# Decoder of two layers, self-attentions: the maxima carried to the query rows by halves, exponentials 12 slots behind

## What is computed

```python
# layer 0: 16 heads of 16, causal
scores = jnp.einsum('bhqd,bhkd->bhqk', q, k) * scale
scores = jnp.where(causal, jnp.finfo(scores.dtype).min, scores)
attn = jax.nn.softmax(scores, axis=-1)
out = jnp.einsum('bhqk,bhkd->bhqd', attn, v)

# layer 1: two sets of 16 heads of 8, not causal, subtracted
scores = jnp.einsum('bthd,bshd->bhts', qh, kh) * SCALE
p = jax.nn.softmax(scores, axis=-1)
a = attn1 - lam * attn2
```

## Time and profile before

| | us |
|---|---|
| median of 3 runs | 3518.33 |
| lowest, highest | 3510.25, 3528.14 |
| the profiled execution | 3509.75 |
| its span on the core | 3508.0 |
| layer 0, first reduction to last combination of maxima | 133.8 to 579.9 |
| layer 1, first to last combination of maxima | 1316.2 to 2488.9 |

### The profile page before, as it was taken

One profiled execution on the slowest core, in us unless ns is written; L12 is line 12 of the kernel. 1 busy time (PEld: TensorE's weight loads), 2 busy tenths in 40 slices (PEclk: granted clock), 3 DMA queues, 4 the chain that ended last, 5 costly groups with the idle time before them and its releaser, 6 DMA issues. The chain is left out here.

```text
span 3508.0 us, 63576 instructions
## 1 busy us (share of the span) xinstructions
PE 3154.7 (90%) x23976; PEld 1627.2 (46%) x23976; DVE 2774.6 (79%) x4723; ACT 2106.0 (60%) x4204; POOL 874.1 (25%) x1302
## 2 busy tenths in 40 slices
PE   7599999678499879999999999999958699999699
PEld 4244444444288533333333333333346445454556
DVE  7788985447577799999999999999367677776456
ACT  3178887245333217999999999999927333334130
POOL 4234333134333430000000000000023344445100
PEclk9699999879699978999999999999979899999789
DMA  5422220000000240100100100100002411100001
GB/s 181 134 54 62 57 57 21 27 1 1 25 1 1 96 137 20 29 20 20 30 20 21 29 20 20 30 20 20 2 7 110 155 43 39 38 26 1 17 1 48
DMA packets 69411, 143.97 MB, mean 41 GB/s; under 512 B 20752, under 2 KB 33872, under 8 KB 68976
## 3 DMA queue, kind: packets, MB, share of 16 engines
q1 hardware_dynamic: 64752, 135.71, 13.0%
q10 hardware_dynamic: 4352, 4.20, 0.4%
HBM read 83.08 MB, written 54.53 MB: 39 GB/s over the span
## 5 line engine op out<-in xcount | busy, mean ns | idle before, releaser
L600 ACT ACTIVATE L_parts<-L_attn_psS 128x512 f32<-128x512 f32 (+3 forms) x2816 | 1407.9, 574 | 144.1 <-PE L_attn_psS L727 109.9
L683 DVE TENSOR_REDUCE L_attn_tops<-L_attn_psM 128x2 f32<-128x1024 f32 x1152 | 1325.0, 1215 | 53.5 <-PE L_attn_psM L777 49.7
L777 PE MATMUL L_attn_psM<-L_K,L_Q 30*128 30x512 f32 (+4 forms) x2816 | 864.7, 488 | 62.1 <-DVE L_attn_tops L683 27.2
L727 PE MATMUL L_attn_psS<-L_Q,L_K 32*128 32x512 f32 (+4 forms) x2816 | 876.7, 473 | 2.2 <-ACT L_parts L600 1.0
L748 PE MATMUL L_attn_psS<-L_parts,L_attn_V 128*32 128x256 f32 (+1 forms) x10752 | 851.8, 389 | 5.9 <-ACT L_parts L600 0.6
L727 PEld LDWEIGHTS L_attn_psS<-L_Q,L_K 32*128 32x128 f32 (+1 forms) x2816 | 409.4, 184 | 552.7 <-ACT L_parts L600 264.6
L777 PEld LDWEIGHTS L_attn_psM<-L_K,L_Q 30*128 30x128 f32 (+1 forms) x2816 | 391.5, 189 | 109.1 <-DVE L_attn_tops L683 59.8
L748 PEld LDWEIGHTS L_attn_psS<-L_parts,L_attn_V 128*32 128x32 f32 x10752 | 214.3, 108 | 353.9 <-issue 184.3
L677 DVE CUSTOM_DVE_ANT_0 L_attn_psM<-L_attn_psM,L_attn_wide 128x384 f32<-128x384 f32 (+3 forms) x512 | 236.6, 522 | 18.7 <-PE L_attn_psM L777 18.1
L2294 ACT ACTIVATE x_E<-x_psS 128x512 f32<-128x512 f32 x256 | 138.9, 595 | 179.9 <-PE x_psS L2417 177.8
L2340 DVE TENSOR_REDUCE x_tops<-x_psM 128x2 f32<-128x1024 f32 x128 | 153.4, 1206 | 92.1 <-PE x_psM L2446 91.9
(11 more groups left out here) (363 smaller groups left out, 4073.9 us busy)
## 6 DMA issues: line engine op xcount, KB each, us to landing
parts_q<-L_parts SPq DMA_DIRECT2D x64, 256.0 KB
parts_k<-L_parts SPq DMA_DIRECT2D x64, 256.0 KB
L_Q<-parts_q SPq DMA_DIRECT2D x192, 64.0 KB
L_K<-parts_k SPq DMA_DIRECT2D x192, 64.0 KB
L_Q<-parts_q SPq DMA_DIRECT2D x64, 128.0 KB
L_K<-parts_k SPq DMA_DIRECT2D x64, 128.0 KB
queries<-x1p_qo SPq DMA_DIRECT2D x16, 512.0 KB, 3.8
keys<-x1p_ko SPq DMA_DIRECT2D x16, 512.0 KB, 4.3
```

The source lines that it names most:

```text
L600: act.activation(E[(4 * n + s) % (4 * RING)][:, c0:], psS[bank][:, c0:], ACT.Exp, scale=scale).then_inc(e_done, 1)
L683: dve.tensor_reduce(dst, src, AX, ALU.max).then_inc(m_read, 1)
L727: pe.matmul(psS[bank][:, c0:], K[g.slot][r:r + RH, c, kt * P:(kt + 1) * P], Q[g.slot][r:r + RH, c, q * HALF + c0:(q + 1) * HALF], start=Tr ...
L777: last = pe.matmul(psM[bank][:, j * HALF:j * HALF + n], Q[t.slot][r:r + TOP, c, qt * P:(qt + 1) * P], K[t.slot][r:r + TOP, c, h * HALF:h * ...
```

## The change

It splits the way of the maxima by query halves and shortens the lag.

- `pairs` is now ordered by halves: all pairs with query tiles 0 to 3 (`of_half[0]`: 8 in layer 0, 16 in layer 1), then those with 4 to 7. Layer 0's hand-made order of blocks goes.
- `LAG` is the number of slots from a group's first pair to its first exponential: max(8/2 + 4, 12 + 4 - 4) = 12 in layer 0 and max(16/2 + 4, 16 + 4 - 8) = 12 in layer 1, where it was 17 and 21.
- For each half: `combine` is one tensor_tensor maximum of 16 columns (not negated; `K` holds -1.0 in the rows instead), `turn_maxima` one transposition, `maxima` one copy on ACT, `cut` a rounding copy and a subtraction on POOL, and SP's `rows` four DMAs in layer 0 and two in layer 1 (each fills the half row of two or four heads). These stand in the slots T_AT: slot 4 and slot 12 in layer 0, 8 and 16 in layer 1.
- `combine` stands between the slot's two reductions and waits for reductions up to the last of its half alone. The wait of the next group's reductions on it goes to the first pair of each half, for the same half of the group before.
- PE waits for the rows of a half before the first score of that half: slot 12 for both layers' first half, slot 16 (layer 0) and 20 (layer 1) for the second.
- SP's order becomes: rows of the second half of g - 1, load of g + 1, rows of the first half of g.
- The two halves' `turn_back` and `back` stand at slots 18 and 27 after the group's start in layer 0, 22 and 30 in layer 1.

```diff
-                    pool.memset(K[k][:].bitcast(F32), 1.0).then_inc(blank, 1)
+                    pool.memset(K[k][:].bitcast(F32), -1.0).then_inc(blank, 1)
...
-        blocks = [(4, 0), (5, 0), (3, 0), (0, 0), (7, 1), (4, 1), (6, 0), (7, 0), (2, 0), (1, 0), (6, 1), (5, 1)]
+            blocks = [(0, 0), (3, 0), (1, 0), (2, 0)] if q == 0 else [(t, h) for t in range(4, TB) for h in range(2)]
...
-    LATE = 5
+    of_half = [sum(t // 4 == q for _, t, _, _, _ in pairs) for q in range(2)]
+    LATE = 4
+    LAG = max(of_half[0] // 2 + LATE, NS + LATE - (ends[0] + 1))
...
-    BACK1, BACK0 = LATE + BACK + 1, LATE + ends[0] + BACK + 3 - BACK
+        B_AT = [LAG + BACK + ends[0] + 3 - BACK, LAG + BACK + ends[1] + 2]
+        SLOTS = groups * NS + B_AT[1] - NS + 4
+        T_AT = [of_half[0] // 2, NS]
+        SUM_AT = LAG + BACK
...
+                def rows(g, q):
+                    sp.wait_ge(m_cut, 2 * (2 * g + q) + 2)
+                    for j in range(2):
+                        for c in range(NQ):
+                            to = Q[g % 3][TOP + j:TOP + j + (HP - 1) * RH + 1:RH, c, q * HALF:(q + 1) * HALF]
+                            src = mparts[q][g % 2][c * 4 * HP:(c + 1) * 4 * HP, j, :]
+                            sp.dma_start(to.bitcast(F32), src.bitcast(F32)).then_inc(mx[q][g % 2], 16)
+                load_group(sp, keep, dh, 1)
+                for g in range(groups):
+                    if g >= 1:
+                        rows(g - 1, 1)
+                        if g + 1 < groups:
+                            if g >= 2:
+                                sp.wait_ge(s_done, s_at[g - 2, NS - 1, 3] + 1)
+                            load_group(sp, keep, dh, g + 1)
+                    rows(g, 0)
...
+                def cut(g, q):
+                    pt, done = mparts[q][g % 2], 2 * (2 * g + q)
+                    pool.wait_ge(e_done, freed["T", g, q])
+                    pool.tensor_copy(pt[:, 0, :], mT[q][g % 2][:]).then_inc(m_cut, 1)
+                    pool.wait_ge(m_cut, done + 1)
+                    pool.tensor_tensor(pt[:, 1, :], mT[q][g % 2][:], pt[:, 0, :].bitcast(F32), ALU.subtract).then_inc(m_cut, 1)
...
-                    act.activation(mparts[k][:, 0, :], psS[bank][0:4 * TB, 0:P], ACT.Copy).then_inc(m_cut, 1)
-                    act.activation(mT[k][:], psS[bank][0:4 * TB, 0:P], ACT.Copy).then_inc(e_done, 1)
+                    act.activation(mT[q][g % 2][:], psS[bank][0:16, 0:P], ACT.Copy).then_inc(e_done, 1)
...
-                    dve.wait_ge(m_read, m_item(t.base, NP2 - 1)[0] + 1)
-                    dve.tensor_reduce(negm[t.slot][:], tops[:], AX, ALU.max, negate=True).then_inc(m_neg, 1)
+                    dve.wait_ge(m_read, m_item(g, of_half[0] * (1 - q) + NP2 * q - 1)[0] + 1)
+                    dve.tensor_tensor(most_of[q][g % 2][:], tops[:, q, :, :, 0], tops[:, q, :, :, 1], ALU.max).then_inc(m_most, 1)
...
+                for slot in range(SLOTS):
+                    new = at(slot, 0)
                     if new:
+                        reduce(new[0], 2 * new[1])
+                    for q in range(2):
+                        if event(slot, T_AT[q]):
+                            combine(group(slot, T_AT[q]), q)
                     if new:
+                        reduce(new[0], 2 * new[1] + 1)
...
+                    for q in range(2):
+                        if exp and exp[1] == (ends[0] + 1) * q:
+                            pe.wait_ge(mx[q][exp[0] % 2], ROWS * (exp[0] // 2 + 1))
+                    for s in range(4):
+                        if exp:
+                            score(*exp, s)
+                        if new:
+                            most(new[0], 2 * new[1] + s // 2, 1 - s % 2)
+                        if (s + 1) * HALVES % 4 == 0 and summed:
+                            product(*summed, (s + 1) * HALVES // 4 - 1)
```

More of the change, by code:

```diff
@@ L354, in attend @@
     TOP = RH - 2
+    ROWS = 2 * NQ * 16
     head = lambda s: (s // HP, RH * (s % HP))
@@ L434, in cuts, with event, group @@
+        def event(slot, offset):
+            return slot >= offset and (slot - offset) % NS == 0 and (slot - offset) // NS < groups
+        def group(slot, offset):
+            return (slot - offset) // NS
+        T_AT = [of_half[0] // 2, NS]
+        SUM_AT = LAG + BACK
         def cuts(g, n):
-            return g.times(4 * sum(diagonal), 4 * sum(diagonal[:n]))
-        def in_turn(new, last):
-            return range(NS if new or last else LATE + BACK + 4)
+            return g * 4 * sum(diagonal) + 4 * sum(diagonal[:n])
@@ new lines, in attend @@
+        for slot in range(SLOTS):
+            exp, summed = at(slot, LAG), at(slot, SUM_AT)
+            if exp:
+                left += [exp + (s,) for s in range(4)]
+                taken += [exp + (s,) for s in range(2)]
+            if summed and (summed[1] == 0 or summed[1] - 1 in ends):
+                taken.append(("O", summed[0], steps[summed[1]][0]))
+            if exp:
+                taken += [exp + (s,) for s in range(2, 4)]
+            for q in range(2):
+                if event(slot, T_AT[q]):
+                    taken.append(("T", group(slot, T_AT[q]), q))
+                    left.append(("T", group(slot, T_AT[q]), q))
+            if summed and summed[1] in ends:
+                left.append(("O", summed[0], steps[summed[1]][0]))
+            for q in (1, 0):
+                if event(slot, B_AT[q]):
+                    taken.append(("B", group(slot, B_AT[q]), q))
+                    left.append(("B", group(slot, B_AT[q]), q))
@@ L516, in _ @@
+                rows(groups - 1, 1)
+                for q in range(2):
+                    for k in range(2):
+                        sp.wait_ge(mx[q][k], ROWS * (groups // 2))
             @block.gpsimd
@@ L563, in trim @@
                         pool.affine_select(block, block, [[1, P]], ALU.is_ge, 0.0, base=0, channel_multiplier=-1).then_inc(e_cut, 1)
-                def turn(t, new, last, old):
-                    if new:
-                        copy(t)
-                    for n in in_turn(new, last):
-                        g, k, live = (t.base - 1, n - LATE, last) if n >= LATE else (t.base - 2, NS + n - LATE, old)
-                        if live and diagonal[k]:
-                            trim(g, k)
-                        if last and n == 0:
-                            cut(t.base - 1)
-                        if old and n == 1:
-                            normalise(t.base - 2, 0)
-                        if old and n == BACK1 + 2:
-                            normalise(t.base - 2, 1)
-                run(turn)
+                for slot in range(SLOTS):
+                    if event(slot, 0):
+                        copy(group(slot, 0))
+                    if at(slot, LAG) and diagonal[at(slot, LAG)[1]]:
+                        trim(*at(slot, LAG))
+                    for q in range(2):
+                        if event(slot, T_AT[q]):
+                            cut(group(slot, T_AT[q]), q)
+                    for q in (1, 0):
+                        if event(slot, B_AT[q] + 2):
+                            normalise(group(slot, B_AT[q] + 2), q)
                 pool.wait_ge(o_norm, 2 * groups)
@@ L621, in evacuate @@
                     act.activation(oT[q][:], psS[bank_of["O", g, q]][:], ACT.Copy).then_inc(e_done, 1)
[L623 to L641 removed]
+                for slot in range(SLOTS):
+                    if at(slot, LAG):
+                        exps(*at(slot, LAG))
+                    for q in range(2):
+                        if event(slot, T_AT[q]):
+                            maxima(group(slot, T_AT[q]), q)
+                    for q in range(2):
+                        if event(slot, SUM_AT + ends[q]):
+                            evacuate(group(slot, SUM_AT + ends[q]), q)
+                    for q in (1, 0):
+                        if event(slot, B_AT[q]):
+                            back(group(slot, B_AT[q]), q)
             @block.vector
             def _(dve):
[L645 removed]
+                dve.memset(tops[:], LOWEST).then_inc(t_blank, 1)
                 if causal:
@@ L752, in product @@
                         last.then_inc(o_done, 1)
-                def products(t, n, last, old, half):
-                    j = n - LATE - BACK
-                    if j >= 0 and last:
-                        product(t.base - 1, j, half)
-                    if j < 0 and old:
-                        product(t.base - 2, NS + j, half)
                 def turn_back(g, q):
```

272 lines of the change are left out of this document (93 added, 179 removed).

## The result

| | before | after |
|---|---|---|
| median | 3517.14 us | 3507.43 us |
| lowest, highest | 3510.14, 3528.14 | 3492.87, 3514.91 |
| ratio (95% interval) | | 0.9966 (0.9954 to 0.9978) |
| span of the profiled execution | 3508.0 | 3509.2 |

A forecast was written before the change was run, and what follows sets the result against it. It took DVE's back-to-back reductions to bound layer 1, and no engine to be full in layer 0. Terms -21.1 + 0.5 - 5 + 0 = -25.6 us, so 3518.3 - 26 = 3492 us, range 3474 to 3522.

The forecast's parts named there:

- Layer 1, the tail: Layer 1 after the last combination: LAG 12 instead of 21 takes nine slots of four exponentials out, -21.1 us.
- Layer 1, the fill: Layer 1's first group: nine slots now shared with exponentials, +0.5 us; the earlier lower-clock stretch priced at nothing.
- Layer 1, the groups: Layer 1, each group: 37.5 against 37.8 us from DVE's rows; -0.15 taken, bounds -0.4 to +0.4, x 32 = -5 us.
- it is not PE that sets the pace: Layer 1's steady stretch: PE's busy figure is modelled; two back-to-back DVE reductions of 1.13 us set each slot.
- rival (b): PE holds DVE up at both layer-1 transpositions (+13 us), layer 0's order costs its upper bound (18): 3520 us; chance 0.22.
- The rows: Query rows due 3 slots after transposition: 4.3 of 7.1 us in layer 1, 5.7 of 6.7 in layer 0; wait nothing.
- rival (c): Layer 0: the second half's row late in every group, 26 to 38 us, kernel slower at 3518 to 3541; chance 0.13.
- (d): The lag isn't effective because the first half's maxima wait for the load; nothing moves, 3518 us; chance 0.02.
- Layer 0, the groups: Layer 0, each group: 28.6 against 28.1 us, +0.5, bounds -0.6 and +1.2; x 15 = +7.5 us.
- sum of slot maxima: Layer 0's group priced slot by slot by its longest engine: 28.1 before (28.11 measured), 28.6 after.
- Layer 0, the tail: Layer 0's end, from the tail's first slot: 34.5 us instead of 44.1, -9.6 us, keeping the clock's fall.
- The combination beside GpSimd: Layer 0: the two-input DVE combination may wait for POOL's 0.29 us trim, up to 5 us higher; left out of sum.

The follow-up runs named there:

- the omission: Three of four transpositions back left out in both layers, in the kernel before and in the kernel after: 3495.47 and 3488.41 us, one execution each.

## Why the prediction was partly right, and where it was wrong

**Layer 1, the tail: right.** -21.1 predicted, -21.4 measured, of which 1.1 is only the place of the last combination in the order. With the old lag it is 52.1 again.

**Layer 1, the fill: this step failed.** I priced the shift of the stretch at lower clock at nothing, "once in both kernels, only earlier". It occurs once, but it is longer. From the first exponential to the rise 11.6 us passed before and 24.1 after. Windows of after, the last without exponentials, the first with them, and the last two of that stretch:

```profile
1301.00:1305.00 4.00, 2.99 (x9) 1.07 (x7) 4.00 (x4) 0.00 (x0) 0.00 (x0) 0.50 0.01 4
1305.00:1309.00 4.00, 4.00 (x20) 1.50 (x19) 4.00 (x5) 3.37 (x6) 0.00 (x0) 0.50 0.00 0
...
1325.00:1329.00 4.00, 4.00 (x32) 1.28 (x28) 2.97 (x3) 2.52 (x5) 0.00 (x0) 0.50 0.42 127
1329.00:1333.00 4.00, 4.00 (x46) 1.50 (x44) 3.49 (x5) 3.41 (x7) 0.00 (x0) 0.95 0.23 70
```

With exponentials at 0.50 DVE has 2.5 to 3.1 of 4 us, as in the earlier trace rows, but now in five windows instead of two. Without them it is full even at 0.50, so what lies between the first exponential and the rise is paid. The price can be read from four kernels with the lag of 12: from the stage's start to c1 they need 82.3, 83.6, 84.3 and 85.9 us, with 18.8, 22.3, 24.1 and 27.6 us between first exponential and rise, some 0.4 us for each microsecond. The 12.5 us more of after are then some 5 us, an estimate from these four. Term: +0.5 predicted, +6.5 measured (1.1 of it c0's place, so 5.4 by the change). In layer 0 the same: the rise came 14.4 us after the first exponential before, 23.4 after, and c0 to c1 grew by 4.2, where +2.0 was predicted for the whole fill. Layer 0 changed alone had the rise after 12.7 and c0 to c1 30.9; layer 1 of after with the omission had it after 11.6 and c0 to c1 37.9. Why the delay is longer with the short lag is not shown.

**Layer 1, the groups: this step failed by more.** -5 predicted (-0.15 x 32), +11.4 measured (+0.38 x 30), at my upper bound of +0.4. Timeline of DVE after, one half (compare):

```profile
1892.81 3.56 DVE L678 TENSOR_REDUCE L_attn_tops<-L_attn_psM 128x2 f32<-128x1024 f32 x3 [0.33 <-PE L_attn_psM L762]
1896.28 0.17 DVE L691 TENSOR_TENSOR L_attn_most<-L_attn_tops 128x16 f32<-128x16 f32 x1
1896.37 1.22 DVE L678 TENSOR_REDUCE L_attn_tops<-L_attn_psM 128x2 f32<-128x1024 f32 x1
1897.50 0.24 DVE L684 RECIPROCAL L_attn_rec<-L_attn_ob 128x16 f32<-128x16 f32 x1
1897.72 13.85 DVE L678 TENSOR_REDUCE L_attn_tops<-L_attn_psM 128x2 f32<-128x1024 f32 x12
1911.89 1.23 DVE L678 TENSOR_REDUCE L_attn_tops<-L_attn_psM 128x2 f32<-128x1024 f32 x1 [0.33 <-PE L_attn_psM L762]
```

The terms that I priced came out, taken together. A combination costs 0.09 from start to start (1896.28 to 1896.37), not 0.16; the reciprocal 0.22, not 0.16; the listed wait at transposing back is the 0.33 that I allowed. With 36.24 for the reductions that is 36.24 + 2 x (0.09 + 0.22 + 0.33) = 37.5, as in the prediction. The group is 38.15. The 0.6 us that are missing are a term which I put at nothing: reductions that start late although no idle time is listed before them. Before the change they were 0.2 us a group (36.24 + 0.46 + 0.32 + 0.24 + 0.33 = 37.6, measured 37.77). One such place, with the pair ahead of it for comparison and PE's matmul that feeds the late one:

```profile
1904.52 3.48 DVE L678 TENSOR_REDUCE L_attn_tops<-L_attn_psM 128x2 f32<-128x1024 f32 x3
1906.78 2.52 DVE L678 TENSOR_REDUCE L_attn_tops<-L_attn_psM 128x2 f32<-128x1024 f32 x2
1908.08 1.23 DVE L678 TENSOR_REDUCE L_attn_tops<-L_attn_psM 128x2 f32<-128x1024 f32 x1
...
1907.51 0.50 PE L762 MATMUL L_attn_psM<-L_K,L_Q 30*128 30x512 f32 x1
```

The reduction at 1908.08 comes 1.30 us after the one at 1906.78, not 1.13, and 0.56 us after the start of its matmul (1907.513 to 1908.078). No reduction of layer 1 starts sooner behind its matmul, so that distance marks where DVE has caught up with PE; elsewhere a reduction starts 0.6 to 1.0 us behind. DVE catches up at three places in each half after, so six a group (behind the reciprocal, at 1908.08 and its like, at the transposing back), and at three a group before. So "it is not PE that sets the pace", on which I built the sum from DVE's rows, is the step that failed: at these places PE sets it. Their number is not the price: with the old lag and the new halves they are four a group, and the group is as long. A half takes 19.08 us (1892.81 to 1911.89) for 16 reductions of 1.13 (18.12): 0.96 is lost, in both halves, 1.9 a group against 1.5 before.

What makes PE late is in part open. The longer groups come with the halves and not with the lag (38.13 with the old lag); 0.23 of the 0.38 goes with the transposition, ACT's copy and their bank half a slot later; for the other 0.15 the runs don't show the cause. The first part of rival (b) had the size (+0.4 x 32 = 13) and 0.22 as its chance, but not the mechanism: it had PE wait for its combination, and against it I said that the combination is ready when PE comes. So it is, by 0.17 us. That rival (b)'s number came true is luck.

**The rows: right.** Among the waits of the kernel before is one of the scores for the query rows, 3.0 us in 5 cases:

```profile
PEld L_attn_psS L727 <- DMA L_Q<-L_attn_mparts: 3.0, 5, 1.0
```

After, no such wait is listed in either layer, so rival (c) did not happen; nor did (d), since the tail is short.

**Layer 0, the groups: sign right, size half.** +0.5 predicted, +0.25 measured (28.09; my sum of slot maxima said 28.6); x 14 that is +3.5 us instead of +7.5. That the old lag leaves 28.14 shows that it is the order and the halves, not what stands beside what. The sum of slot maxima did not hit before either: the 28.11 that it was held against includes the longer distance from c0 to c1, and the groups after it are 27.84 apart. It was 0.2 too high before and 0.5 after; that queues even neighbours out is my reading, not shown.

**Layer 0, the tail: better than predicted, in part by luck.** -9.6 predicted, -14.5 measured. The clock stood at 0.50 for 17 us of the tail before and for 7 after (0.65 and 0.50 in the windows above). Where it did not fall at all, the tail was 38.1 with the old lag and 27.4 with the new one: 10.7 for the five slots. The other 3.8 are the shorter stretch at 0.50. Its length isn't the change's doing alone: in the kernel with the small products added it was 17 us again, with a tail of 32.8.

**The combination beside GpSimd.** The Trainium skill, SBUF — State Buffer, "SBUF: two separate sides", would let the two-input combination wait for GpSimd's operations that read SBUF. In layer 0, where 16 of the 32 combinations run beside a trim, it takes 164 to 176 ns, in layer 1 162 to 176: no such wait shows here, and the up to 5 us that I set beside the sum by that rule are nothing.

**The sum.** Predicted -21.1 + 0.5 - 5 and -9.6 + 2.0 + 7.5 = -25.7. Measured -21.4 + 6.5 + 11.4 and -14.5 + 4.4 + 3.5 = -10.1. Layer 1's groups (16 us off) and its fill (6 off) are the miss, and layer 0 (6.6 better) covered part of it. The time lay in the range 3474 to 3522, but the range was wide enough for no gain at all.

## What to carry to other kernels

When a small operation that crosses engines is split in two, count its whole way twice: not the 0.1 us of the instruction, but what it adds to each engine's order. A sum over the fullest engine's rows holds only while that engine never catches up with the one that feeds it: look for starts that come late without a listed idle time. An idle time that a profile puts down to a producer is a wait only if the same spacing isn't there without one; compare it with the kernel that lacks the producer. Moving the consumer half a slot behind was worth 0.23 us in each of 32 groups here, for a reason that isn't shown. A shorter lag takes its slots out of the tail one for one, but starts the heavy work earlier in a stretch of low clock; here that cost some 0.4 us for each microsecond from the first exponential to the rise. Where four banks are all in turn, look at when a bank is taken, not only at when it is used: half a slot more cost 2.4 us a group, where leaving out three quarters of the block behind it gave 0.25.

## What the hardware showed that I had not expected

The granted clock of TensorE rose from 0.50 (1.2 GHz) to 1.00 (2.4 GHz) 8 to 28 us after the first exponential, and PE being shown as busy 4.0 of 4 us well ahead of it, with small products added, did not bring it. With the long lag the delay was 8.1 to 15.1 us, with the short one 15.7 to 27.8, but in two cases 11.6 and 12.7. What decides it stays open: layer 1's rise lay 60 us after the stage's start before and 52 after, so neither the stage's start nor the first exponential fixes it.

A DVE tensor_tensor of 128x16 on two operands in SBUF took 162 to 176 ns and delayed the next reduction by 0.09 us, where one whose data are still on their way out of the same engine (the old combination) cost 0.46. Of the 1024 reductions of 128x1024 in layer 1, before and after, DVE started none less than 0.56 us after the start of the second matmul that feeds it. DVE's wait at a block of four transpositions on PE fell only from 0.33 to 0.21 us when three of four were left out.
